# A cross-attention kernel: queries projected once and scattered by small transfers, keys sent by thirds

## The chip, the cores and the metric

One core of one Trainium2 chip runs the whole program. The metric is the device time of one execution in microseconds (us), median of several. The engines are TensorE (PE), VectorE (DVE), ScalarE (ACT), GpSimd (POOL) and SyncE (SP), which here only issues transfers.

## The reference, cut to what matters

```python
def _L0_xattn_ref(Q, K, V, mask, W_q, W_k, W_v, W_o):     # 32 batches, 100 queries, 1444 keys, width 128, 16 heads of 8
    q = (Q @ W_q.T).reshape(B, -1, 16, 8).transpose(0, 2, 1, 3)
    k = (K @ W_k.T).reshape(B, -1, 16, 8).transpose(0, 2, 1, 3)
    v = (V @ W_v.T).reshape(B, -1, 16, 8).transpose(0, 2, 1, 3)
    scores = jnp.einsum('bhqd,bhkd->bhqk', q, k) / np.sqrt(8)
    attn = masked_softmax(scores, m)                      # clip to +-50, exp, mask, divide by the sum
    out = jnp.einsum('bhqk,bhkd->bhqd', attn, v)
    ...
x = x + _L0_xattn_ref(_layernorm(x), ctx_1024, ctx_1024, mask, W_q, W_k, W_v, W_o)
x = x + _L0_ffn_ref(_layernorm(x), gate_w, w1, w2)        # 8 experts of width 512, the best two of each token
```

## The kernel before

**Batches and chunks.** The attention runs over 32 batches. The keys of a batch lie in 12 tiles of 128, the heads in 4 groups of 4; a group of one tile gives scores of 128 keys x 400 (4 heads x 100 queries). Three such blocks make a chunk, so a batch has 16 chunks, numbered c = 0 to 15. For each chunk PE makes the scores into one of two PSUM halves (line 689), ACT takes the exponential (line 899), and DVE clips it (`clip`, line 1047). On every even chunk PE also runs 24 matmuls that weigh the values with the clipped exponentials of earlier chunks (`weigh_values`, line 701); odd chunks have none.

**The steps between.** After the scores of each chunk PE does one step of `STEPS`, which all go through one PSUM bank, `scratch`. A step may start only when ACT or DVE has emptied the bank of the step before (`scratch_emptied`). During batch b the steps prepare batch b+1 (`PREPARE`: query, turn and key for each third of the keys, value for each third) and finish batch b-1 (`FINISH`: heads, queries, project, tokens, gate, rank). The order before is turn, key, turn, key, turn, key, heads, queries, project, query, value, tokens, gate, value, value, rank, in chunks 0 to 15. So turn steps stand in even chunks, followed by the 24 matmuls, and key steps in odd ones. PE runs in order: a step that waits holds up the scores behind it.

**Scores from split operands.** The score matmuls read the type fp32r. Each operand is split by DVE into a rounded part and a rest (`split_keys`, `split_queries`), and the four products of the parts are summed by stacking them along the 128 rows of the contraction: 4 terms x 4 heads x 8. The keys get there by transfer: `stack_keys` issues 16 transfers of 192 KB per batch on SP's queue (line 405), one for each term and group, once all three thirds are split. The queries are projected four times over, from a weight in which each group's columns are repeated for the four terms (`wq_rep`, `project_q`, line 624: four matmuls, which the profile shows as eight instructions). POOL then multiplies them with `head_mask`, which leaves each row only its own head's columns, and writes `q_stack`, 128 x 1600 (`stack_queries`, line 505).

**Who waits for the stacks.** The scores of chunk 0 of the next batch are made in chunk 15 of this one. Ahead of them PE waits for `q_stacked` and for all 16 transfers of `k_stacked`. SP's order in a batch is: wait for all scores of the batch before, load the context for two batches on, fill rows of the expert buffer (line 397), wait for the three key splits, send the 16 transfers. Ahead of batch 0 the same is done alone (`ALONE`, `first_keys`), and `xT` is built from normalised tokens.

POOL's other work in a batch is small: line 560 and 562 (the deviation of the second norm), which DVE waits for two chunks after project, and the sending of routed rows by indirect transfers (line 570), which follows rank. DVE takes the gate's logits at line 1100.

After the attention come the experts, 57 tiles of 128 rows, and the final sums; the diff leaves them alone.

## Time and profile before

| | |
|---|---|
| median of 3 runs | 1222.54 us (1222.02 to 1223.01) |
| profiled execution, its own time | 1220.12 us |
| its span | 1218.4 us |
| PE / DVE / ACT / POOL busy | 1074.9 / 860.4 / 753.7 / 366.9 us |
| transfers on SP's queue | 84084 packets, 152.55 MB |
| POOL's stack of the queries (L505) | 32 times, 107.4 us busy |

The span runs from the first to the last instruction of the profiled execution; its own time holds 1.7 us more. Busy times of different engines overlap, so they don't add up to the span. In a timeline "x8" merges eight instructions in a row, "[1.37 <-X]" is the idle time of that engine just before, and what ended it. The busy time of a matmul includes its way through the array, so that neighbours overlap by some 0.15 us; the distance between two starts is what an instruction group takes on PE.

### The profile page before, as it was taken

What the parts mean: (1) busy time and instruction counts of PE and PEld (TensorE: products, weight loads), DVE (VectorE), ACT (ScalarE), POOL (GpSimd) and SP (SyncE); (2) the same over time, 40 slices, a digit from 0 to 9 for tenths busy, and PEclk for the clock granted to TensorE, in tenths of its full rate; (3) what the DMA queues carried; (4) which work ended last, traced back from release to release, by engine and by line L of the source; (5) the groups of instructions that cost most, each with busy time, mean ns of one, the idle gap of its engine ahead of it and who ended that gap; (6) DMA issues with size and microseconds to landing.
All of it is one profiled execution on the core that took longest, in us unless ns stands there. A gap on an engine that the chain in (4) does not pass through costs nothing.

```text
span 1218.4 us, 30948 instructions
## 1 busy us (share of the span) xinstructions
PE 1074.9 (88%) x10734; PEld 778.3 (64%) x10735; DVE 860.4 (71%) x1955; ACT 753.7 (62%) x959; POOL 366.9 (30%) x357
## 2 busy tenths in 40 slices
PE   5699999999999999999999999999999999869990
PEld 3466666666666666666666666666666666569990
DVE  4567777777777777777777777777777777644443
ACT  2576666666666676766666766666666666634440
POOL 3712222222222222222222222222222222235554
PEclk8799999999999999999999999999999999979995
DMA  6655666666555665555555556666666666312225
GB/s 157 144 125 137 143 146 145 145 144 139 133 131 135 145 145 135 134 134 134 134 134 134 132 133 138 145 145 145 145 145 137 134 135 141 113 48 66 68 57 162
DMA packets 89010, 159.58 MB, mean 131 GB/s; under 512 B 13792, under 2 KB 66020, under 8 KB 88980
## 3 DMA queue, kind: packets, MB, share of 16 engines
q1 hardware_dynamic: 84084, 152.55, 54.3%
q0 software_dynamic: 4896, 6.63, 2.0%
q8 instruction: 18, 0.29, 0.1%
q14 instruction: 12, 0.10, 0.0%
HBM read 36.83 MB, written 22.08 MB: 48 GB/s over the span
## 4 chain that ended last, share of the span: by engine, by line
PE 64%; DVE 17%; ACT 5%; issue 5%; SPq 4%; DMA 4%; ACTq 0%; DVEq 0%; POOL 0%; POOLq 0%
PE o_sum L701 17%; PE scores L689 15%; DVE probs L1047 12%; PE scratch L618 6%; PE scratch L632 6%; PE scratch L613 5%; ACT k_full L866 4%; PE scores L805 4%; PE scores L816 4%; SPq L405 3%; PE scratch L624 2%; DVE v_both L983 2%; PE scratch L662 2%; DMA k_stack<-k_lo 2%; DMA x_all<-in_x_dram 1%
## 5 line engine op out<-in xcount | busy, mean ns | idle before, releaser
L899 ACT ACTIVATE probs<-scores 128x1200 f32<-128x1200 f32 x512 | 589.5, 1179 | 114.9 <-PE scores L689 114.9
L1047 DVE TENSOR_SCALAR probs<-probs 128x1200 f32<-128x1200 f32 x512 | 471.2, 947 | 52.9 <-ACT probs L899 50.4
L689 PE MATMUL scores<-q_stack,k_stack 128*128 128x400 f32 x1536 | 431.3, 395 | 13.4 <-DMA k_stack<-k_lo 11.3
L689 PEld LDWEIGHTS scores<-q_stack,k_stack 128*128 128x128 f32 x1536 | 255.8, 190 | 141.6 <-issue 98.3
L701 PE MATMUL o_sum<-probs,v_both 128*17 128x200 f32 x6144 | 309.8, 334 | 0.1
L701 PEld LDWEIGHTS o_sum<-probs,v_both 128*17 128x17 f32 x6144 | 154.8, 97 | 84.1 <-issue 16.5
L632 PE MATMUL scratch<-w_turned,ctxT 128*128 128x128 f32 x768 | 112.0, 289 | 56.0 <-DVE logits L1100 41.3
L570 POOL DMA_INDIRECT expert_rows<-rows,row_atu x64 | 79.0, 1235 | 264.0 <-DVE row_atu L1140 238.2
L632 PEld LDWEIGHTS scratch<-w_turned,ctxT 128*128 128x128 f32 x768 | 93.8, 192 | 87.3 <-DVE logits L1100 51.3
L505 POOL TENSOR_TENSOR q_stack<-q_parts,head_mask 128x1600 fp32r<-128x1600 f32 x32 | 107.4, 3357 | 96.9 <-DVE q_parts L970 96.9
L560 POOL TENSOR_SCALAR rstd<-moments 100x1 f32<-100x1 f32 x32 | 39.0, 1220 | 279.5 <-DVE moments L1085 279.5
L866 ACT COPY k_full<-scratch 128x512 f32<-128x512 f32 (+1 forms) x93 | 52.1, 560 | 92.0 <-PE scratch L618 92.0
L618 PE MATMUL scratch<-ctxT,w_turned 128*128 128x512 f32 x186 | 91.1, 571 | 0.0
L957 DVE CAST k_hi<-k_full 128x512 fp32r<-128x512 f32 (+1 forms) x93 | 38.9, 419 | 58.1 <-ACT k_full L866 58.1
L983 DVE COPY v_both<-scratch 128x512 f32<-128x512 f32 x93 | 64.1, 689 | 17.0 <-PE scratch L632 14.8
L596 POOL DMA_INDIRECT expert_outputs<-ctx_nat,tile_home x57 | 56.8, 997 | 61.7 <-DVE ctx_nat L1249 60.1
L959 DVE TENSOR_TENSOR k_lo<-k_full,k_hi 128x512 fp32r<-128x512 f32 (+1 forms) x93 | 61.4, 660 | 3.2
L805 PE MATMUL scores<-ctxT 128*128 128x128 f32 x456 | 61.7, 279 | 0.0
L816 PE MATMUL scores<-w_sb,k_full 128*128 x456 | 60.9, 276 | 0.1
L930 ACT ACTIVATE k_full<-scores 128x512 f32<-128x512 f32 x57 | 34.0, 597 | 38.0 <-PE scores L805 37.4
L805 PEld LDWEIGHTS scores<-ctxT 128*128 128x128 f32 x456 | 56.6, 195 | 0.3
L816 PEld LDWEIGHTS scores<-w_sb,k_full 128*128 128x128 f32 x456 | 55.5, 192 | 0.5 <-issue 0.5
(145 smaller groups left out, 869.8 us busy)
## 6 DMA issues: line engine op xcount, KB each, us to landing
k_stack<-k_hi SPq DMA_DIRECT2D x256, 192.0 KB, 4.6
k_stack<-k_lo SPq DMA_DIRECT2D x256, 192.0 KB, 5.4
expert_rows<-fill SPq DMA_DIRECT2D x32, 406.2 KB
xT_and_ctx<-in_ctx_dram SPq DMA_DIRECT2D x16, 704.0 KB
ctx_nat<-in_ctx_dram SPq DMA_DIRECT2D x16, 704.0 KB
v_both<-expert_rows SPq DMA_DIRECT2D x57, 65.0 KB, 1.8
xT_and_ctx<-in_L_ffn_w_dram SPq DMA_DIRECT2D x1, 2048.0 KB, 11.7
w_sb<-in_L_ffn_w_dram SPq DMA_DIRECT2D x8, 256.0 KB, 7.1
```

Source lines behind the costliest of these rows:

```text
L505: nc.gpsimd.tensor_tensor(q_stack[p][:], q_parts[:].bitcast(F32).unsqueeze(2).broadcast_to([P, GROUPS, HG, SQ]), head_mask[:].unsqueeze(1) ...
L570: nc.gpsimd.indirect_dma_start(out=expert_rows[0:E * CAP, :], out_offset=bass.IndirectOffsetOnAxis(ap=row_atu[:, k:k + 1], axis=0), in_=ro ...
L618: return nc.tensor.matmul(into[:, 0:KEYS[k]], w_turned[:, WK, :], ctxT[:, KEY_COLS[k]], start=True, stop=True)
L632: last = nc.tensor.matmul(scratch[:, j * P:(j + 1) * P], ctxT[:, t * P:(t + 1) * P], w_turned[:, WV, :], start=True, stop=True)
L689: last = nc.tensor.matmul(scores[:, c % 2, m, 0:GQ], k_stack[p][:, g, t * P:(t + 1) * P], q_stack[p][:, g, :, :].rearrange("p h q -> p (h ...
L701: last = nc.tensor.matmul(o_sum[32 * g:32 * g + VW, s * PQ:(s + 1) * PQ], v_ones[p][:, t, 2 * g + s, :], probs[:, c % RING, m, s * PQ:(s + ...
L805: last = nc.tensor.matmul(scores[:, n % 2, 0, c * P:(c + 1) * P], w1_tile[:, n % 2, c * P:(c + 1) * P], tileT[:, n % 2, :], start=True, st ...
L816: last = nc.tensor.matmul(scores[:, n % 2, 1, 0:D], hiddenT[:, n % 2, c, :], w2_sb[:, bass.ds(expert, 1), c, :].rearrange("f o d -> f (o d)"),
L866: nc.scalar.copy(k_full[:, k, 0:KEYS[k]], scratch[:, 0:KEYS[k]]).then_inc(scratch_emptied, 1)
L899: nc.scalar.activation(probs[:, c % RING, :, :], scores[:, c % 2, :, 0:GQ], ACT.Exp, scale=SCALE).then_inc(exp_ready, 1)
L983: nc.vector.tensor_copy(v_ones[p][:, k * KC:(k + 1) * KC, :, 0:2 * DH], scratch[:].rearrange("p (t n d) -> p t n d", t=KC, n=PAIRS)).then_ ...
L1047: nc.vector.tensor_scalar(chunk, chunk, LOW, HIGH, ALU.max, ALU.min).then_inc(probs_ready, 1)
```

## The change

The queries are projected once, 128 x 100, and split in two parts (`q_parts`, 128 x 2 x 100). `q_stack` is zeroed once by POOL, and 16 transfers of 12.5 KB (8 rows of 4 x 100 numbers, in pieces of 400 bytes) write the blocks that aren't zero. POOL's product, `head_mask` and `wq_rep` go. With it goes an order of columns in which one transfer takes a term for all groups: the columns of `W_q` and `W_k` are put in the order head, place in the head, group when ACT copies the turned weights. The keys are sent a third at a time, 4 transfers of 256 KB in pieces of 2 KB, each third as soon as it is split and with a semaphore of its own; PE waits for the second and third in the chunks that first need them. The query step moves from chunk 9 to chunk 0. The order is then query, turn, key, turn, key, turn, key, heads, queries, project, value, value, tokens, gate, value, rank.

```diff
@@ constants
-    KD = 16 * 4 * GROUPS
+    KD = 16 * 4
+    QD = 16 * 4 * HG
...
-    STEPS = (PREPARE[1:7] + FINISH[:3] + PREPARE[:1] + PREPARE[7:8] + FINISH[3:5] + PREPARE[8:] + FINISH[5:])
+    STEPS = PREPARE[:7] + FINISH[:3] + PREPARE[7:9] + FINISH[3:5] + PREPARE[9:] + FINISH[5:]
@@ SP
-            def stack_keys(p):
+            def stack_keys(p, b):
                 R = HG * DH
-                for t, part in enumerate((k_hi, k_lo, k_hi, k_lo)):
-                    for g in range(GROUPS):
-                        sp.dma_start(k_stack[p][t * R:(t + 1) * R, g, :].bitcast(F32),
-                                     part[g * R:(g + 1) * R, :].bitcast(F32)).then_inc(k_stacked, 16)
+                for k in range(KSTEPS):
+                    sp.wait_ge(k_split, KSTEPS * b + k + 1)
+                    cols = slice(k * KC * P, (k + 1) * KC * P)
+                    for t, part in enumerate((k_hi, k_lo, k_hi, k_lo)):
+                        sp.dma_start(k_stack[p][t * R:(t + 1) * R, :, cols].bitcast(F32),
+                                     part[:, cols].bitcast(F32)).then_inc(k_stacked[k], 16)
+            def stack_queries(p):
+                R = GROUPS * DH
+                for t in range(4):
+                    for h in range(HG):
+                        first = t * HG * DH + h * DH
+                        sp.dma_start(q_stack[p][first:first + DH, :, h, :].bitcast(F32),
+                                     q_parts[h * R:(h + 1) * R, t // 2, :].bitcast(F32)).then_inc(q_stacked, 16)
             sp.wait_ge(cleared, 3)
-            sp.wait_ge(k_split, KSTEPS)
-            stack_keys(0)
+            stack_keys(0, 0)
+            sp.wait_ge(q_stack_cleared, 2)
+            sp.wait_ge(q_split, 1)
+            stack_queries(0)
...
                 fill_rows(b + 1)
-                sp.wait_ge(k_split, KSTEPS * (b + 2))
-                stack_keys(1 - p)
+                sp.wait_ge(q_split, b + 2)
+                stack_queries(1 - p)
+                stack_keys(1 - p, b + 1)
@@ POOL
-            nc.gpsimd.memset(own_head[:], 1.0).then_inc(own_head_step, 1)
...
+            for p in range(2):
+                nc.gpsimd.memset(q_stack[p][:].bitcast(F32), 0.0).then_inc(q_stack_cleared, 1)
...
-            def stack_queries(p, b):
...
-                nc.gpsimd.tensor_tensor(
-                    q_stack[p][:], q_parts[:].bitcast(F32).unsqueeze(2).broadcast_to([P, GROUPS, HG, SQ]),
-                    head_mask[:].unsqueeze(1).unsqueeze(3).broadcast_to([P, GROUPS, HG, SQ]), ALU.mult
-                ).then_inc(q_stacked, 1)
@@ PE
-                for g in range(GROUPS):
-                    last = nc.tensor.matmul(scratch[:, g * SQ:(g + 1) * SQ],
-                                            wq_rep[:, g, :, :].rearrange("p t r -> p (t r)"),
-                                            xT[:, cols], start=True, stop=True)
+                last = nc.tensor.matmul(scratch[:, 0:SQ], w_turned[:, WQ, :], xT[:, cols], start=True, stop=True)
...
+                        for k in range(1, KSTEPS):
+                            if c + 1 == k * KC * GROUPS // CB:
+                                pe.wait_ge(k_stacked[k], KD * (b + 1))
                         score_chunk(p, c + 1)
                     elif not last_one:
-                        pe.wait_ge(q_stacked, b + 2)
-                        pe.wait_ge(k_stacked, KD * (b + 2))
+                        pe.wait_ge(q_stacked, QD * (b + 2))
+                        pe.wait_ge(k_stacked[0], KD * (b + 2))
@@ ACT
-            nc.scalar.copy(w_turned[:].rearrange("p n d -> p (n d)"), scores[:, 1, 2, :]
+            nc.scalar.copy(w_turned[:, 0:2, :].rearrange("p n (h d g) -> p n h d g", h=HG, d=DH),
+                           scores[:, 1, 2, 0:2 * P].rearrange("p (n g h d) -> p n h d g", n=2, g=GROUPS, h=HG))
+            nc.scalar.copy(w_turned[:, 2:4, :].rearrange("p n d -> p (n d)"), scores[:, 1, 2, 2 * P:4 * P]
...
-            nc.scalar.copy(wq_rep[:], w_turned[:, WQ, :].rearrange("p (g r) -> p g r", g=GROUPS)
...
-                    nc.scalar.copy(q_full[:], scratch[:, 0:GROUPS * SQ]).then_inc(scratch_emptied, 1)
+                    nc.scalar.copy(q_full[:], scratch[:, 0:SQ]).then_inc(scratch_emptied, 1)
@@ DVE
-                    dve.wait_ge(k_stacked, KD * b)
+                    dve.wait_ge(k_stacked[k], KD * b)
...
-                    dve.wait_ge(q_stacked, b)
-                flat = q_parts[:].rearrange("p g q -> p (g q)")
-                nc.vector.tensor_copy(flat, q_full[:]).then_inc(q_hi_ready, 1)
+                    dve.wait_ge(q_stacked, QD * b)
+                nc.vector.tensor_copy(q_parts[:, 0, :], q_full[:]).then_inc(q_hi_ready, 1)
                 dve.wait_ge(q_hi_ready, b + 1)
-                nc.vector.tensor_tensor(flat[P // 2:P, :], q_full[P // 2:P, :],
-                                        flat[P // 2:P, :].bitcast(F32), ALU.subtract
+                nc.vector.tensor_tensor(q_parts[:, 1, :], q_full[:], q_parts[:, 0, :].bitcast(F32), ALU.subtract
                                         ).then_inc(q_split, 1)
```

## Rows read from the trace of the kernel before

**Rows 1.** The page: busy time of each engine over the whole span.

```profile
PE 1074.9 (88%) x10734; PEld 778.3 (64%) x10735; DVE 860.4 (71%) x1955; ACT 753.7 (62%) x959; POOL 366.9 (30%) x357
```

**Rows 2.** Busy time by stretch: PE, PEld, DVE, ACT, POOL, then PE clock, DMA share, GB/s.

```profile
23.00:40.80 17.80, 5.63 (x24) 4.79 (x25) 12.91 (x72) 2.06 (x4) 13.54 (x17) 0.50 0.95 206
587.00:619.00 32.00, 29.65 (x307) 20.59 (x306) 24.62 (x52) 21.78 (x26) 8.42 (x7) 1.00 0.60 138
```

**Rows 3.** Timeline of PE over one batch: start us, us, engine, line, operation.

```profile
577.71 0.25 PE L671 MATMUL scratch<-ident,rows 100*128 100x100 f32 x1
...
581.88 1.16 PE L632 MATMUL scratch<-w_turned,ctxT 128*128 128x128 f32 x8 [1.37 <-DVE logits L1100]
...
583.95 1.16 PE L632 MATMUL scratch<-w_turned,ctxT 128*128 128x128 f32 x8 [0.36 <-DVE v_both L983]
585.04 1.21 PE L701 MATMUL o_sum<-probs,v_both 128*17 128x200 f32 x24
...
586.83 0.26 PE L682 MATMUL scratch<-chosen,before 100*100 100x8 f32 x2
...
587.75 0.60 PE L613 MATMUL scratch<-ident,xT_and_ctx 128*128 128x128 f32 x4
...
590.07 1.02 PE L618 MATMUL scratch<-ctxT,w_turned 128*128 128x512 f32 x2
...
591.84 0.66 PE L613 MATMUL scratch<-ident,xT_and_ctx 128*128 128x128 f32 x4 [0.20 <-ACT k_full L866]
...
599.98 0.65 PE L662 MATMUL scratch<-ident,o_raw 128*100 128x128 f32 x4
...
603.01 0.38 PE L667 MATMUL scratch<-w_turned,attnT 128*100 128x128 f32 x2
...
605.12 1.03 PE L624 MATMUL scratch<-xT_and_ctx,wq_rep 128*128 x8
...
606.80 1.16 PE L632 MATMUL scratch<-w_turned,ctxT 128*128 128x128 f32 x8
...
609.68 0.25 PE L671 MATMUL scratch<-ident,rows 100*128 100x100 f32 x1
```

**Rows 4.** The waits: us in total, times, longest.

```profile
PE scratch L632 <- DVE logits L1100: 41.3, 30, 1.4
```

**Rows 5.** Timeline of DVE, then of POOL, in the same batch.

```profile
577.62 4.14 DVE L1047 TENSOR_SCALAR probs<-probs 128x1200 f32<-128x1200 f32 x2
...
601.17 0.36 DVE L1064 TENSOR_TENSOR attn<-scratch,rden 100x64 f32<-100x64 f32 x2
...
577.75 3.37 POOL L505 TENSOR_TENSOR q_stack<-q_parts,head_mask 128x1600 fp32r<-128x1600 f32 x1 [2.93 <-DVE q_parts L970]
```

**Rows 6.** Line 1047 alone: duration in ns, min/median/max.

```profile
L1047 DVE TENSOR_SCALAR probs<-probs x512: 752/779/3439, 43.5 to 1057.2; 128x1200 f32<-128x1200 f32 x171
```

**Rows 7.** Timeline of ACT in the same batch.

```profile
588.39 0.58 ACT L862 COPY ctxT<-scratch 128x512 f32<-128x512 f32 x1
```

**Rows 8.** Timeline of the lead-in, all engines.

```profile
9.82 0.23 POOL L515 TENSOR_SCALAR rstd<-moments 100x4 f32<-100x4 f32 x1 [6.72 <-DVE moments L1005]
...
19.85 0.69 DVE L993 TENSOR_TENSOR k_lo<-scores,k_hi 128x512 fp32r<-128x512 f32 x1
...
23.08 2.53 SPq L405 DMA_DIRECT2D k_stack<-k_hi  x4
...
28.70 0.57 DVE L970 TENSOR_TENSOR q_parts<-q_full,q_parts 64x400 fp32r<-64x400 f32 x1
...
32.35 2.92 SPq L405 DMA_DIRECT2D k_stack<-k_lo  x4
...
40.83 1.67 PE L689 MATMUL scores<-q_stack,k_stack 128*128 128x400 f32 x4 [10.44 <-DMA k_stack<-k_lo]
```

**Rows 9.** Lines 397 and 384 on SP's queue: one issue in ns; issue to landing.

```profile
L397 SPq DMA_DIRECT2D expert_rows<-fill x32: 315/324/1120, 36.0 to 999.5; - x32
...
DMA to landing us min/median/max: 1.8/2.0/2.1
```

More of the change, by code:

```diff
@@ L163, in xattn_moe @@
         w_turned = sb("w_turned", [P, 4, P])
-        wq_rep = sb("wq_rep", [P, GROUPS, 4, HG * DH])
-        q_parts = sb("q_parts", [P, GROUPS, SQ], F32R)
-        own_head = sb("own_head", [P, 4, HG])
-        head_mask = sb("head_mask", [P, HG])
+        q_parts = sb("q_parts", [P, 2, SQ], F32R)
         q_stack = [sb(f"q_stack{p}", [P, GROUPS, HG, SQ], F32R) for p in range(2)]
@@ L176, in xattn_moe @@
         k_full = sb("k_full", [P, KSTEPS, KC * P])
-        q_full = sb("q_full", [P, GROUPS * SQ])
+        q_full = sb("q_full", [P, SQ])
         k_hi = sb("k_hi", [P, TILES * P], F32R)
@@ L282, in xattn_moe @@
         xT_ready = sem("xT_ready")
-        wq_rep_ready = sem("wq_rep_ready")
-        own_head_step = sem("own_head_step")
-        head_mask_ready = sem("head_mask_ready")
+        q_stack_cleared = sem("q_stack_cleared")
         q_hi_ready = sem("q_hi_ready")
@@ L293, in xattn_moe @@
         q_split = sem("q_split")
-        k_stacked = sem("k_stacked")
+        k_stacked = [sem(f"k_stacked{k}") for k in range(KSTEPS)]
         scores_ready = sem("scores_ready")
@@ L489, in _ @@
                                     base=0, pattern=[[-1, P]], channel_multiplier=1).then_inc(ident_ready, 1)
-            nc.gpsimd.memset(own_head[:], 1.0).then_inc(own_head_step, 1)
-            pool.wait_ge(own_head_step, 1)
-            nc.gpsimd.affine_select(out=own_head[:], in_=own_head[:], compare_op=ALU.is_ge, fill=0.0, base=0,
-                                    pattern=[[-HG * DH, 4], [-DH, HG]], channel_multiplier=1
-                                    ).then_inc(own_head_step, 1)
-            pool.wait_ge(own_head_step, 2)
-            nc.gpsimd.affine_select(out=own_head[:], in_=own_head[:], compare_op=ALU.is_ge, fill=0.0, base=DH - 1,
-                                    pattern=[[HG * DH, 4], [DH, HG]], channel_multiplier=-1
-                                    ).then_inc(own_head_step, 1)
-            def stack_queries(p, b):
-                pool.wait_ge(q_split, b + 1)
-                if later(b, 2):
-                    pool.wait_ge(scores_ready, CHUNKS * (b - 1))
-                nc.gpsimd.tensor_tensor(
-                    q_stack[p][:], q_parts[:].bitcast(F32).unsqueeze(2).broadcast_to([P, GROUPS, HG, SQ]),
-                    head_mask[:].unsqueeze(1).unsqueeze(3).broadcast_to([P, GROUPS, HG, SQ]), ALU.mult
-                ).then_inc(q_stacked, 1)
+            for p in range(2):
+                nc.gpsimd.memset(q_stack[p][:].bitcast(F32), 0.0).then_inc(q_stack_cleared, 1)
             pool.wait_ge(half_ready, 1)
@@ L537, in _ @@
                 invert_deviations(r)
-            pool.wait_ge(head_mask_ready, 1)
-            stack_queries(0, 0)
             for r in range(DVE_NORMS, QSTEPS):
@@ L576, in during @@
                     invert_deviation(b - 1)
-                if not (isinstance(b, int) and b == B - 1):
-                    stack_queries(1 - p, b + 1)
                 if later(b):
@@ L730, in _ @@
                     pe.wait_ge(xT_ready, 1)
-                    pe.wait_ge(wq_rep_ready, 1)
                 into_scratch(name, k, 0, 0, None, step)
@@ L735, in _ @@
             pe.wait_ge(mask_ready, 1)
-            pe.wait_ge(q_stacked, 1)
-            pe.wait_ge(k_stacked, KD)
+            pe.wait_ge(q_stacked, QD)
+            pe.wait_ge(k_stacked[0], KD)
             score_chunk(0, 0)
@@ L847, in _ @@
                 nc.scalar.copy(ctxT[:, KEY_COLS[k]], scores[:, 0, k, 0:KEYS[k]]).then_inc(ctxT_ready, 1)
-            act.wait_ge(w_turned_ready, 1)
-            nc.scalar.copy(wq_rep[:], w_turned[:, WQ, :].rearrange("p (g r) -> p g r", g=GROUPS)
-                           .unsqueeze(2).broadcast_to([P, GROUPS, 4, HG * DH])).then_inc(wq_rep_ready, 1)
             def take(name, k, b, f, step):
@@ L1017, in _ @@
             nc.vector.tensor_copy(mask_rows[:], mask_u8[:]).then_inc(mask_cast, 1)
-            dve.wait_ge(own_head_step, 3)
-            nc.vector.tensor_reduce(head_mask[:], own_head[:].rearrange("p t h -> p h t"), AX.X, ALU.add
-                                    ).then_inc(head_mask_ready, 1)
             moments_of(0)
```

## The prediction

> **What bounds the kernel now.** I read the page first. PE is busy for 88% of the span, the next engine for 71% [rows 1], so the question is what PE does in the rest. The windows come second: a steady stretch of 32 us holds 29.65 us of PE at a granted clock of 1.00, that is at the 2.4 GHz level, and the transfer engines are busy for 0.60 of it [rows 2]. So PE bounds the attention, but 2.35 us of each stretch are stalls. Third comes PE's timeline, where the reader should look at distances between starts. The batch repeats from 577.71 to 609.68, so a period is 31.97 us [rows 3]. The largest stall is 1.37 us ahead of a value step, because the gate's logits hadn't been taken from `scratch`; the waits have it 30 times, 41.3 us in all [rows 3, 4].
>
> Why is DVE late with the logits? Its two clips at 577.62 take 4.14 us together. POOL's product for the query stack runs from 577.75 to 581.12, inside them [rows 5]. The middle clip takes 779 ns and the longest 3439 ns [rows 6]: two undisturbed ones would be 1.56 us, so 2.6 us are lost while POOL works, and the first DVE work behind them is the logits. The stall on PE is DVE's loss less the slack that the 24 matmuls of the even chunk give.
>
> **Part 1: POOL's product goes.** The clips fall back to 0.78 us each, and the logits are taken about 2.6 us sooner. That is more than the stall, so all of it goes: 1.37 us in the idle column, or 1.52 by distances. I find the latter so: tokens to value was 581.88 - 577.71 = 4.17 us, and the work in it is one even gap and one odd gap. What an even chunk adds after its step is the 24 matmuls and the next scores: 586.83 - 585.04 = 1.79 us. The 24 matmuls alone are 1.14 (1.21 less their overlap), so the scores are 0.65. With 0.21 for the small tokens and gate matmuls the work is 1.79 + 0.65 + 0.21 = 2.65, and the stall 1.52 [rows 3].
>
> **Part 2: one projection in place of four.** Query to value is 606.80 - 605.12 = 1.68 us: 0.65 scores, some 0.81 of query matmuls, the rest a stall for ACT's copy [rows 3]. A quarter of the matmuls is 0.20 us (0.26 if a quarter of the busy 1.03 counts). ACT's copy and DVE's split shrink too, but lie beside PE's work.
>
> **Part 3: the order of the steps.** Moving query to chunk 0 shifts turn, key, heads, queries and project by one chunk, so each changes between even (covered by the 24 matmuls) and odd (covered by scores alone). I go round the new batch and compare gap by gap [rows 3, 7].
> - Turn to heads, before: 599.98 - 587.75 = 12.23 us. Now turn is odd. Its matmuls take 0.60, ACT's copy starts 0.11 later and takes 0.58 [rows 7], and 0.05 later PE may go on: 1.33 against 0.53 + 0.65 = 1.18 of work, a stall of 0.15. Key is even, and its copy is covered: the stall of 0.20 ahead of each turn goes. A pair is 1.33 + 0.9 (key) + 1.79 = 4.02, twice, and 3.81 for the shorter third: 11.85.
> - Heads to project, before 603.01 - 599.98 = 3.03. Heads is now odd, and DVE's reciprocal and two products of the heads (0.65 us in a row up to 601.53 [rows 5]) with 0.2 of hand-over are longer than the 0.65 of scores. I take a stall of 0.28: 0.57 + 0.65 + 0.28 + 0.02 + 1.79 = 3.31.
> - Project to value, before 606.80 - 603.01 = 3.79 with query in it. Now project is odd: 0.31 + 0.65 + 0.14 of stall = 1.10. Query in chunk 0 is 0.20 + 1.79 = 1.99. Together 3.09.
> - The first value step to the next step is 609.68 - 606.80 = 2.88, as before.
> - From there to the last value step, before 6.24 (4.17 + 583.95 - 581.88 = 2.07 for an odd value step with its stall). Now the odd value step comes first, 2.07, then tokens and gate without the stall, 2.65: 4.72.
> - The last value step to rank 2.88 and rank to the next batch 0.92, both as before.
>
> Before: 12.23 + 3.03 + 3.79 + 2.88 + 6.24 + 2.88 + 0.92 = 31.97, the period. After: 11.85 + 3.31 + 3.09 + 2.88 + 4.72 + 2.88 + 0.92 = 29.65 us. The difference is 2.32 us per batch, made of about 1.5 for POOL, 0.6 for the projection and 0.2 from the rest.
>
> One dependence gets shorter: rank needs `chosen`, which DVE now makes one chunk before it. Behind the last value step DVE copies values (0.7), picks (0.6), and PE has 1.79 until rank: just enough. The share of the gate is now taken by ACT in chunk 15, behind an exponential that by then is done. If it were late, DVE would hold rank, and PE the query step of the next batch.
>
> **Part 4: the transfers.** The 16 query transfers are new on SP's queue. An issue costs 0.32 us when nothing holds it [rows 9], and 2.92 / 4 = 0.73 us among key transfers [rows 8]: 5 to 12 us per batch. The 12 key transfers carry the same 3 MB at 9 to 11 us. With the context and the rows (1 us) SP has 15 to 24 us of issues in 29.65. The queries go first, in chunk 1, the last keys after chunk 7, near 15 us: sent by 19, landed by 26 even with 7 us of landing. Chunk 0 of the next batch needs only the first third, and the last third isn't wanted before chunk 10. So I cost them at nothing. What hides them is PE's batch itself; if the queue ran full, the excess over 29.65 us would be paid. DVE's waits for `q_stacked` and `k_stacked[k]` before it overwrites the parts concern transfers one batch old.
>
> The pieces of a query transfer are 400 bytes, and no SBUF-to-SBUF transfer of such pieces is in the trace; the expert buffer's rows of 520 bytes go in pieces as small and are issued at 0.32 us [rows 9]. I take them as cheap and keep the other end as a rival. The Trainium skill, DMA: Bandwidth & Descriptors, section Bandwidth, says that transfers under 64 KB are descriptor-dominated and gives each a fixed cost of about 2 us. If these costs added up, 16 of them would be 32 us per batch, as an estimate from that page, longer than a batch; the trace speaks against adding them up, for the four weight loads of 64 KB, issued in a row, each landed within 2.1 us of its issue [rows 9].
>
> **Part 5: the lead-in.** PE stands 10.44 us before its first scores, at a clock of 0.50 (the 1.2 GHz level) and with the transfer engines 0.95 busy at 206 GB/s [rows 2, 8]. The keys are sent from 23.08; by thirds they can start at 19.85 + 0.69 = 20.54, so the last key transfer is issued near 32.9 instead of 35.3. Behind it SP issues 16 query transfers (their split is ready by 29.3), 5.1 us at best and 11.7 at worst, and they land 2 us later: first scores at 40 to 46.6 us instead of 40.83 [rows 8, 9]. The keys at least thin out by then; I take 41.5, a loss of 0.7. The two clearings of `q_stack` cost at most a product of the same size each, 6.7 us together, and lie in POOL's idle 6.72 us ahead of 9.82 [rows 5, 8]; cover gone, they would delay that line by a few us once.
>
> **The sum.** The POOL stall is there in 30 batches [rows 4], so I take 30 x 2.32 = 69.6 us. Batch 0 gives about 1 (the projection and half a stall), the last batch prepares nothing. 69.6 + 1 - 0.7 = 70 us. The profiled execution's own time of 1220.1 becomes 1150, and the median of the runs, 1222.5, which is 2.4 above it, becomes 1152.5. I round down to 1152.
>
> **The rivals.**
> - Odd steps drain slower than I reckon. The one odd step with a measured drain by DVE, the value step, stalls PE for about 0.5 us. If turn (three times), heads and project each stalled so, instead of 0.15, 0.15, 0.09, 0.28 and 0.14, that is 1.7 us more per batch, 51 in all: 1203. With half of it 1177. For it: DVE and ACT are both busy for two thirds. Against: DVE loses 2.6 us of waiting. Chance 0.12 for a gain between 20 and 50 us.
> - POOL's product isn't the cause of the slow clips, and something else, such as the key transfers that run at the same time, is. Then only the projection and the order count, 0.8 us per batch: 1222.5 - 25 = 1197. Against: the clip ends with POOL's product and not with the transfers. Chance 0.03.
> - PE loses nearly all stalls: 29.65 less 1.2 is 28.4 us, another 36 us: 1116. Chance 0.06 for anything below 1135.
> - It ends slower: small transfers occupy the queue one after the other. A 64 KB transfer lands 1.8 to 2.1 us after its issue [rows 9]; if each of the 16 held the queue for 1.8 us, they would take 29 us, with 9 for keys and 3 for the context and rows 41 us per batch: 9 us more than before, 31 batches, 1500. It decides from 1.2 us each: 16 x 1.2 + 12 = 31 us. Chance 0.04.
> - No change within 0.2% (2.4 us, about what this measurement can tell): gain and new stalls cancel, 2.3 us of new stalls per batch. Chance 0.02.
>
> **How the numbers follow.** The forecast as described, 1135 to 1172, has 0.73. Leaving out 2 in 10 of all cases, I take 1134 to 1176, which takes in the lead-in's bounds (-1 to +6), the query matmuls' (0.06 x 31 = 2 us), and a third of the first rival. Faster 0.94, same 0.02, slower 0.04.
>
> **What the profile after would show.** Line 1047's longest instruction near 1 us instead of 3.4. No wait of PE for the logits of 41 us. The query step as two instructions right behind rank. A period of 29 to 30.3 us between two value steps. Stalls of 0.1 to 0.3 us ahead of the key steps for ACT's copy, where they stood ahead of turn. No wait of PE on `k_stack` or `q_stack` outside the lead-in. The first scores at 40 to 47 us. I would be wrong if the key step waited for a copy that stands behind an exponential, if rank came late because `chosen` is made one chunk before it, or if SP were still issuing query transfers when the keys are split.

## The result, and the profile after

The changed kernel takes 1331.46 us (median of 4 runs, 1328.71 to 1335.89) where the kernel before takes 1222.28 beside it: a ratio of 1.0899 (95% interval 1.0883 to 1.0915), slower by 9%. The forecast was 1152, in a range of 1134 to 1176. The profiled execution has a span of 1326.7 us at a mean granted clock of 0.917 (1 is the 2.4 GHz level); before they were 1218.4 and 0.972.

A period (the distance between the first and the last of the 14 context loads of one buffer, divided by the 26 batches between them) was (939.2 - 106.6) / 26 = 32.02 us and is (1035.1 - 114.0) / 26 = 35.43. So 30 batches lost 102 us, and the first scores, at 51.54 us instead of 40.83, another 10.7: together 113, where the runs lost 109 (1331.46 - 1222.28).

The page of the changed kernel: busy time of each engine; then its chain that ended last, by engine and by line; then its key transfers (how many, KB each, median us from issue to landing).

```profile
PE 1117.3 (84%) x10542; PEld 792.0 (60%) x10543; DVE 754.8 (57%) x1954; ACT 755.6 (57%) x959; POOL 255.5 (19%) x324
...
SPq 49%; DMA 23%; PE 17%; issue 5%; DVE 5%; ACT 0%; POOL 0%; DVEq 0%; POOLq 0%; ACTq 0%
...
k_stack<-k_hi SPq DMA_DIRECT2D x192, 256.0 KB, 11.6
k_stack<-k_lo SPq DMA_DIRECT2D x192, 256.0 KB, 13.1
```

Against [rows 1] DVE lost 106 us of work and POOL 111, as the change intends. But the chain now runs through SP's queue (`SPq`, the issuing of transfers) and the transfers themselves for 72% of the span, and through PE for 17%, where it was 64% before. PE's busy time even rose by 42 us with fewer matmuls. The waits of PE (us in total, times, longest) say what it waits for:

```profile
PE scores L675 <- DMA k_stack<-k_lo: 96.9, 30, 5.1
PE scores L675 <- DMA q_stack<-q_parts: 22.6, 1, 22.6
```

The wait for the logits of [rows 4] is gone; 96.9 us for the first third of the next batch's keys stand in its place. SP's timeline over one batch and the start of the next shows why they are late (L412 issues queries, L403 keys, L373 the context):

```profile
577.46 20.90 SPq L412 DMA_DIRECT2D q_stack<-q_parts  x16
598.49 0.59 SPq L403 DMA_DIRECT2D k_stack<-k_hi  x1
...
605.72 0.63 SPq L403 DMA_DIRECT2D k_stack<-k_lo  x1
611.30 0.37 SPq L373 DMA_DIRECT2D xT_and_ctx<-in_ctx_dram  x1
...
614.37 18.82 SPq L412 DMA_DIRECT2D q_stack<-q_parts  x16
633.32 0.59 SPq L403 DMA_DIRECT2D k_stack<-k_hi  x1
```

The 16 query issues occupy SP for 18.8 to 20.9 us, and the keys go only then: in the second batch shown DVE had split the first third by 621.85 and the last by 628.20, and SP sent them from 633.32 on. The chain resolves these 16 issues one by one:

```profile
577.46 10.14 SPq L412
587.65 0.71 SPq L412
...
600.42 8.74 DMA k_stack<-k_lo
609.21 1.37 PE scores L675 x3
614.37 2.50 SPq L412
616.91 6.28 SPq L412
623.24 0.67 SPq L412
```

One issue is held for 10.14 us (two, for 2.50 and 6.28, in the next batch); the others follow each other at a distance of 0.71. And the fourth key transfer, the last of the first third, takes 8.74 us to land. Windows of the changed kernel (busy time of PE, PEld, DVE, ACT and POOL, then PE clock, DMA share, GB/s; the share is the mean busy share of the 16 transfer engines and can read a little over 1):

```profile
606.00:611.00 5.00, 1.79 (x8) 1.74 (x8) 0.00 (x0) 0.30 (x1) 0.00 (x0) 0.81 1.08 125
611.00:614.40 3.40, 3.40 (x30) 2.26 (x29) 2.84 (x12) 2.20 (x3) 1.17 (x2) 0.50 1.10 123
618.00:624.00 6.00, 5.87 (x64) 3.42 (x64) 4.41 (x8) 4.98 (x7) 0.00 (x0) 1.00 1.12 127
624.00:630.00 6.00, 5.81 (x54) 3.69 (x56) 3.89 (x9) 4.73 (x8) 0.51 (x2) 1.00 0.84 222
```

Two things are to be seen. The transfer engines are fully busy and move 123 to 127 GB/s, where the lead-in before had 206 at a share of 0.95 [rows 2]. The 3 MB of a batch's keys take 25 us at that rate, by estimate; sent from 598.49 they are through near 623.5. The held query issue goes on at 623.24, and the last window has 222 GB/s: the keys are gone by then. And after PE's stall of 4.05 us the clock falls to the 1.2 GHz level (0.50), where the steady stretch before has 1.00. This is where PE's extra busy time comes from: the same 10542 matmuls are busy for 1060.4 us in experiment 1, which has no such stalls.

So keys and queries follow each other: some 25 us of key traffic until the queries are let in (598.49 to 623.24), then 10.1 us of query issues (623.24 to 633.32) until the keys are let in. From one batch's first key issue to the next these are 34.83 us, in the batch after it 35.37 (633.32 to 668.69), against a measured mean period of 35.43.

### The profile page after: what moved, and what is told of

Read it like the earlier page. It is cut to its first block, busy times and chain, and to the rows that moved or that the text cites. A ratio compares the mean times of both kernels' runs of the same rounds, so it can differ in the third digit from the quotient of the medians.

```text
span 1326.7 us, 31018 instructions
## 1 busy us (share of the span) xinstructions
PE 1117.3 (84%) x10542; PEld 792.0 (60%) x10543; DVE 754.8 (57%) x1954; ACT 755.6 (57%) x959; POOL 255.5 (19%) x324
## 4 chain that ended last, share of the span: by engine, by line
SPq 49%; DMA 23%; PE 17%; issue 5%; DVE 5%; ACT 0%; POOL 0%; DVEq 0%; POOLq 0%; ACTq 0%
SPq L412 43%; DMA k_stack<-k_lo 20%; SPq L403 5%; PE scores L675 4%; PE scores L793 4%; PE scores L804 4%; PE o_sum L687 1%; DVE probs L1028 1%; DMA x_all<-in_x_dram 1%; SPq L474 1%; DMA q_stack<-q_parts 1%; PE scratch L669 1%; DVE q_parts L955 1%; DVE q_parts L953 1%; PE scores L783 0%
## 5 line engine op out<-in xcount | busy, mean ns | idle before, releaser
L675 PE MATMUL scores<-q_stack,k_stack 128*128 128x400 f32 x1536 | 436.1, 396 | 120.9 <-DMA k_stack<-k_lo 96.9
L1028 DVE TENSOR_SCALAR probs<-probs 128x1200 f32<-128x1200 f32 x512 | 388.9, 781 | 82.5 <-ACT probs L885 81.8
L675 PEld LDWEIGHTS scores<-q_stack,k_stack 128*128 128x128 f32 x1536 | 265.7, 202 | 216.9 <-DMA k_stack<-k_lo 107.3
L687 PE MATMUL o_sum<-probs,v_both 128*17 128x200 f32 x6144 | 334.0, 353 | 0.5 <-issue 0.4
L687 PEld LDWEIGHTS o_sum<-probs,v_both 128*17 128x17 f32 x6144 | 161.1, 101 | 149.9 <-issue 84.2
L618 PE MATMUL scratch<-w_turned,ctxT 128*128 128x128 f32 x768 | 105.7, 281 | 1.9 <-ACT v_both L874 0.7
L848 ACT COPY ctxT<-scratch 128x512 f32<-128x512 f32 (+1 forms) x93 | 52.2, 561 | 95.1 <-PE scratch L602 95.1
L607 PE MATMUL scratch<-ctxT,w_turned 128*128 128x512 f32 x186 | 99.7, 618 | 7.4
L1033 DVE COPY o_raw<-o_sum 128x400 f32<-128x400 f32 x32 | 18.4, 575 | 120.0 <-PE o_sum L687 120.0
L545 POOL COPY rows<-home 100x2 f32<-100x2 f32 x32 | 10.3, 320 | 345.7 <-DMA expert_rows<-rows,row_atu 322.6
L551 POOL TENSOR_SCALAR rstd<-moments 100x1 f32<-100x1 f32 x32 | 19.2, 599 | 191.6 <-DVE moments L1066 191.6
## 6 DMA issues: line engine op xcount, KB each, us to landing
q_stack<-q_parts SPq DMA_DIRECT2D x512, 12.5 KB
```

The source lines that it names most:

```text
L607: return nc.tensor.matmul(into[:, 0:KEYS[k]], w_turned[:, WK, :], ctxT[:, KEY_COLS[k]], start=True, stop=True)
L618: last = nc.tensor.matmul(scratch[:, j * P:(j + 1) * P], ctxT[:, t * P:(t + 1) * P], w_turned[:, WV, :], start=True, stop=True)
L675: last = nc.tensor.matmul(scores[:, c % 2, m, 0:GQ], k_stack[p][:, g, t * P:(t + 1) * P], q_stack[p][:, g, :, :].rearrange("p h q -> p (h ...
L687: last = nc.tensor.matmul(o_sum[32 * g:32 * g + VW, s * PQ:(s + 1) * PQ], v_ones[p][:, t, 2 * g + s, :], probs[:, c % RING, m, s * PQ:(s + ...
L1028: nc.vector.tensor_scalar(chunk, chunk, LOW, HIGH, ALU.max, ALU.min).then_inc(probs_ready, 1)
```

## The experiments

Ratios are against the kernel before, run beside it on the same chip, with 95% intervals; the chips differ between experiments, so compare ratios and not times. "Period" is as above. Line numbers shift a little between kernels. A "wait for `k_stack`" is a wait of PE before its scores until keys have landed.

**1. The changed kernel without its query transfers in the loop.** Both stacks are filled once, with the queries of batch 0, so later batches use wrong queries; all else is as in the changed kernel.

```
+            stack_queries(1)
...
-                sp.wait_ge(q_split, b + 2)
-                stack_queries(1 - p)
```

> The changed kernel without the 16 query transfers of each batch (both query stacks are filled once, from batch 0's queries, so all later scores use the wrong queries; everything else runs). In the changed kernel SP spends 18.8 to 20.9 us of each batch on these issues and sends the keys only behind them. Theory A (the query transfers hold the queue and push the keys behind the start of the next batch): PE's waits on k_stack outside the lead-in go from 97 us to under 5, the period falls from 36 us to 29.5 to 30.5, the run to 1150 to 1175 us. Theory B (the keys in pieces of 2 KB are slow by themselves, 24 us of transfers per batch, and fill the batch whatever the queries do): the waits on k_stack stay above 40 us and the run above 1250.

Measured: 1185.88 us, 0.9666 (0.9646 to 0.9685), period 30.23, no wait of PE for `k_stack`, although keys still take a median of 9.8 us from issue to landing (12.3 in the changed kernel). Without the query issues the slow keys harm nobody. The period is the one that theory A gave; the time is 11 us above its range. Some 4 us of that are the lead-in: 32 query transfers are issued there instead of 16, and the first scores come at 55.62 us instead of 51.54. This also isolates the forecast of PE's work: 30.23 against 29.65.

**2. Keys by thirds on the kernel before.** 12 transfers, each from 128 partitions into 32, as in the changed kernel; queries and order as before.

```
+                for k in range(KSTEPS):
+                    sp.wait_ge(k_split, KSTEPS * b + k + 1)
...
+                        sp.dma_start(k_stack[p][t * R:(t + 1) * R, :, cols].bitcast(F32),
+                                     part[:, cols].bitcast(F32)).then_inc(k_stacked[k], 16)
```

> The kernel before with one part of the change alone: the keys by thirds, 12 transfers of 256 KB in pieces of 2 KB (and the columns of W_k in the order they need). POOL's product, four projections and the old order stay. Theory B: the key transfers run at about 125 GB/s here too, where 16 transfers in pieces of 6 KB run at 215, so transfers are busy for over 0.8 of a batch; PE doesn't notice, because the first third goes 8 us earlier: 1190 to 1225 us. Theory A's stronger form (the slow rate is caused by the small query transfers beside them): the rate stays above 190 GB/s, the transfer share at 0.6, 1190 to 1222 us. The rate tells them apart, not the time.

Measured: 1219.03, 0.9928 (0.9911 to 0.9946), period 32.13. The same window columns, for this kernel:

```profile
630.00:640.00 10.00, 9.92 (x120) 7.41 (x114) 7.69 (x16) 7.10 (x10) 3.45 (x3) 1.00 1.08 136
```

136 GB/s with engines at 1.08 and no query transfer anywhere: the rate belongs to the form of the key transfers. So it isn't the small query transfers beside them. The period didn't gain; the first scores came 3 us earlier (37.80).

**3. Keys in 4 whole transfers.** On the changed kernel: the same 128 partitions into 32, but pieces of 6 KB, sent after the third split.

```
+                sp.wait_ge(k_split, KSTEPS * (b + 1))
...
+                    sp.dma_start(k_stack[p][t * R:(t + 1) * R, :, :].bitcast(F32),
+                                 part[:, :].bitcast(F32)).then_inc(k_stacked, 16)
```

> The changed kernel with each term's keys in one transfer of 768 KB in pieces of 6 KB, sent once all three thirds are split (4 transfers; rows still come from all 128 partitions). If the length of the pieces sets the rate: 215 GB/s, 15 us for 3 MB, the query issues aren't held (16 x 0.71 = 11.4 us); the keys are split about 16 us after chunk 15's scores and land 16 us later, so the period is 32 to 34 us and the run 1220 to 1270. If what slows them is that the rows of one transfer come from 128 partitions: 125 GB/s as in the changed kernel, 24 us from the split to the landing, a period near 41 us and 1400 to 1500.

Measured: 1731.77, 1.4111 (1.4086 to 1.4136), period 47.81, beyond what either theory allowed (the mean granted clock is 0.821). A window:

```profile
655.00:662.00 7.00, 4.97 (x65) 3.59 (x65) 4.49 (x14) 3.65 (x5) 0.00 (x0) 1.00 1.05 115
```

Three times longer pieces don't help, nor do three times larger transfers: 115 GB/s. PE waits 439.4 us for the keys, 28 times.

**4. Keys in 16 whole transfers.** As 3, with the transfers of the kernel before, each from 32 partitions into 32.

```
+                    for g in range(GROUPS):
+                        sp.dma_start(k_stack[p][t * R:(t + 1) * R, g, :].bitcast(F32),
+                                     part[g * R:(g + 1) * R, :].bitcast(F32)).then_inc(k_stacked, 16)
```

> The changed kernel with the keys sent as before: 16 transfers of 192 KB in pieces of 6 KB, each from 32 partitions to 32, once all thirds are split. Both readings of the slow rate expect 215 GB/s here. Theory B in full (only the slow keys hurt, the query transfers are free): 1190 to 1215. Theory A and B together (query issues of 11.4 us ahead of the keys, and the keys land 32 to 33 us after chunk 15's scores): 1225 to 1270.

Measured: 1341.43, 1.0924 (1.0904 to 1.0944), period 35.35. A window, then SP's timeline:

```profile
640.00:646.00 6.00, 5.76 (x70) 4.25 (x70) 4.37 (x9) 3.02 (x5) 1.58 (x2) 1.00 1.03 209
```
```profile
622.07 11.88 SPq L411 DMA_DIRECT2D q_stack<-q_parts  x16
634.65 2.57 SPq L402 DMA_DIRECT2D k_stack<-k_hi  x4
...
643.06 3.08 SPq L402 DMA_DIRECT2D k_stack<-k_lo  x4
```

The rate is back (209 GB/s), and the query issues are no longer held: 11.88 us for 16. The time isn't, and lies above both expectations, for another reason: the third split ends at 634.63, the keys are issued at once, until 646.14, and the next scores start 5.8 us later, at 651.98. The cure of the rate was joined to a wait for all thirds, so this run shows the rate and the hold, and not the price.

**5. The new order alone**, on the kernel before.

```
-    STEPS = (PREPARE[1:7] + FINISH[:3] + PREPARE[:1] + PREPARE[7:8] + FINISH[3:5] + PREPARE[8:] + FINISH[5:])
+    STEPS = PREPARE[:7] + FINISH[:3] + PREPARE[7:9] + FINISH[3:5] + PREPARE[9:] + FINISH[5:]
```

> The kernel before with the new order of the steps alone (query in chunk 0). The fourth run's reading is that with the keys sent whole, a chain binds: scores of chunk 0, third split, 16 transfers one behind the other, next scores. Before it took 14.8 + 16.3 = 31.1 us, just under PE's 31.97. The new order puts the third split one chunk later, by 2 us: 33 to 34 us per batch and 1255 to 1290 us, with PE waiting for k_stack or q_stack's semaphores in each batch. Rival (the order costs nothing, as the prediction had it, and the query transfers were what made the fourth run slow): 1205 to 1225.

Measured: 1295.69, 1.061 (1.0589 to 1.0631), period 34.10. Its timelines of DVE, PE and POOL:

```profile
615.95 3.69 DVE L1047 TENSOR_SCALAR probs<-probs 128x1200 f32<-128x1200 f32 x1
...
620.81 0.43 PE L671 MATMUL scratch<-ident,rows 100*128 100x100 f32 x1 [2.33 <-DVE v_both L983]
...
616.16 2.84 POOL L505 TENSOR_TENSOR q_stack<-q_parts,head_mask 128x1600 fp32r<-128x1600 f32 x1
```

The expectation was wrong in its cause, and low in its range: PE waits for `k_stack` only 4 times in the loop, 4.7 us in all. POOL's product stands in POOL's program behind `rstd`, which needs the project step. So it doesn't run right behind the query step in chunk 0, but behind project; it slows a clip ahead of a value copy now, and PE waits 2.33 us for that copy at tokens (69.9 us in 30 times). The clock falls to 0.56 behind it, where 24 matmuls take 2.20 us instead of 1.21. In the kernel before, the order isn't neutral, but what made it dear is POOL's product, which the change removes: with the product on DVE and the keys by thirds the new order costs 0.17 us per batch (experiment 10).

**6. The product on DVE**, on the kernel before, as four instructions of 128x400 each.

```
+                for h in range(HG):
+                    ins = nc.vector.tensor_scalar(q_stack[p][:, :, h, :], q_parts[:].bitcast(F32),
+                                                  head_mask[:, h:h + 1], None, ALU.mult)
```

> The kernel before with the product of the query stack made by DVE, in four instructions of 128 x 400, one for each head of a group, in place of POOL's one. If POOL's product is what stretches the two clips (prediction, part 1): no clip over 1.5 us, PE's wait for the logits goes from 41 us to under 5, and the period falls until the key chain of 31.1 us binds: 1190 to 1207. If something else stretches the clips: they stay at 3.4 us and the run at 1222 or above, since DVE has 1.5 us more work.

Measured: 1220.93, 0.9994 (0.9978 to 1.001), period 32.02: no change. Its line of the clips (duration in ns, min/median/max), then PE's longest wait:

```profile
L1040 DVE TENSOR_SCALAR probs<-probs x512: 751/778/1035, 44.3 to 1058.0; 128x1200 f32<-128x1200 f32 x171
```
```profile
PE scores L674 <- DMA k_stack<-k_lo: 39.1, 29, 10.5
```

The cause of the slow clips is shown: nothing but POOL's product was moved, and the longest clip falls from 3439 ns [rows 6] to 1035. The wait for the logits goes too. But the time stays, above the 1190 to 1207 expected. All keys are still sent after the third split (in one batch from 603.68 until 614.87, and the scores that need them start at 620.70), and PE now waits for them where it had waited for the logits: 10.5 us in the lead-in and 28.6 in 28 batches. A second chain lay directly under the first.

**7. Experiment 6 with keys by thirds** in 12 transfers, as in 2.

> The sixth run's kernel, and the keys by thirds in 12 transfers of 256 KB from 128 partitions. Both bounds are taken away: the lock and the key chain. Period 30.2 to 30.8, transfers busy over 0.9 of it at 125 GB/s in the key stretches: 1165 to 1190 us. If the transfers then bind (24 us of keys, 5 us of context and rows, and they rarely start at once), PE waits for k_stack and it stays at 1195 or above.

Measured: 1181.47, 0.9669 (0.9652 to 0.9687), period 30.80, no wait for `k_stack`. Both are as expected. Thirds and the product's removal are each worth nearly nothing (0.7%, and 0.1% within the noise) and together 3.3%.

**8. Experiment 6 with keys by thirds in 48 transfers** of 64 KB, 32 partitions into 32, pieces of 2 KB as in the changed kernel.

```
+                        for g in range(GROUPS):
+                            sp.dma_start(k_stack[p][t * R:(t + 1) * R, g, cols].bitcast(F32),
+                                         part[g * R:(g + 1) * R, cols].bitcast(F32)).then_inc(k_stacked[k], 16)
```

> As the seventh, but each third in 16 transfers of 64 KB, each from 32 partitions to 32, in pieces of 2 KB; 48 per batch. If it is the spread of a transfer's rows over 128 partitions that halves the rate: above 185 GB/s in the key stretches, transfer share about 0.65, no wait for k_stack, 1165 to 1190 us. If it is the length of the pieces: 125 GB/s again. If the issues of 48 transfers on SP's queue cost 0.6 us each (29 us), SP binds: 1200 or more.

Measured: 1306.4, 1.0685 (1.0666 to 1.0705), period 34.59. A window, and the key issues (ns, min/median/max):

```profile
625.00:630.00 5.00, 4.37 (x47) 3.18 (x46) 4.60 (x16) 4.07 (x5) 0.00 (x0) 1.00 0.42 105
```
```profile
L408 SPq DMA_DIRECT2D k_stack<-k_hi x768: 507/591/2306, 22.3 to 1128.1; - x192
```

105 GB/s with engines at 0.42 is 250 GB/s while they are busy: pieces of 2 KB are not slow, the spread over partitions is. SP, at 0.62 us for each of 48 issues, is the bound now, the third of the outcomes expected: DVE waits 130.0 us, in 32 times, for the key transfers before it may overwrite `k_hi`, and PE waits for DVE. The Trainium skill, DMA: Bandwidth & Descriptors, section Why small descriptors are slow (HBM only), says that transfers between SBUF places don't suffer from small pieces; by that rule, this trace agrees, for pieces of 2 KB.

**9. The changed kernel with its query transfers issued by POOL's own queue**, in loop and lead-in.

```
-                        sp.dma_start(q_stack[p][first:first + DH, :, h, :].bitcast(F32),
+                        nc.gpsimd.dma_start(q_stack[p][first:first + DH, :, h, :].bitcast(F32),
```

> The changed kernel with its 16 query transfers issued by POOL on its own queue instead of SP's; nothing else changes. SP then sends each third of the keys when it is split. If it was their place on SP's queue that cost the time (0.67 us of SP each, and the first one held up by the key transfers before it): no wait for k_stack outside the lead-in, period 30 to 31 us as without the queries (1185.9), run 1170 to 1205. If the transfer engines, busy for 0.9 of a batch with the slow form of the keys, are what the query transfers overload: waits for k_stack or q_stack stay and the run is 1230 or more.

Measured: 1195.17, 0.9747 (0.9726 to 0.9767), period 30.85, no wait for `k_stack`. POOL's timeline:

```profile
611.00 9.94 POOL L496 DMA_DIRECT2D q_stack<-q_parts  x16
```

The same bytes in the same pieces cost 0.62 us per batch against no query transfers at all (30.85 against 30.23) when they don't stand between the keys on one queue, and 5.2 when they do. PE waits for `q_stack` in four batches of the loop, 9.6 us in all.

**10. Experiment 7 with the new order.**

> The seventh run's kernel (product by DVE, keys by thirds in 12 transfers) in the new order of the steps. The order cost 74 us in the fifth run. If that was only the key chain, which the thirds take away, it costs nothing here, and by the prediction's gaps it gives 0.2 us per batch: 1168 to 1185 against 1181.5. If odd steps drain slower than reckoned (the prediction's first rival): 1190 to 1230.

Measured: 1189.45, 0.9705 (0.9676 to 0.9733), period 30.97 against 30.80. The time falls between the two expectations. The intervals of this ratio and of experiment 7's overlap; the gain of 0.2 us per batch that the prediction gave the order isn't there.

**11. Experiment 7 with keys in 24 transfers** of 128 KB, each from 64 partitions into 32.

```
+                        for g in range(0, GROUPS, 2):
+                            sp.dma_start(k_stack[p][t * R:(t + 1) * R, g:g + 2, cols].bitcast(F32),
+                                         part[g * R:(g + 2) * R, cols].bitcast(F32)).then_inc(k_stacked[k], 16)
```

> The seventh run's kernel with two transfers of 128 KB per term and third, each from 64 partitions to 32 (24 per batch, about 15 us of issues). The rate was 215 to 250 GB/s from 32 partitions and 125 from 128. If it falls with the number of source partitions per target partition: 150 to 190 GB/s when the engines are full, transfer share 0.6 to 0.8. The time is PE's either way: 1175 to 1190.

Measured: 1184.13, 0.9655 (0.9634 to 0.9676), period 30.82, with this rate:

```profile
612.00:616.00 4.00, 3.92 (x43) 3.04 (x38) 2.74 (x7) 2.76 (x4) 1.83 (x2) 1.00 1.10 173
```

173 GB/s lies between the 115 to 136 of 128 partitions and the 209 of 32. The size of a transfer doesn't explain this: 128 KB went at 173 here, 192 KB at 209 (experiment 4) and 256 KB at 136 (experiment 2). Where keys don't bind, it is worth nothing.

**12. The changed kernel with keys in 24 transfers**, as in 11; the query transfers stay on SP ahead of the keys.

> The changed kernel with the keys in two transfers of 128 KB per term and third, each from 64 partitions to 32 (24 per batch), which ran at 170 GB/s instead of 125; the 16 query transfers stay on SP's queue, ahead of the keys. If the loss needs both parts, the query issues and the backlog of slow key transfers that holds the first of them for 10 us, then the queries take 12 us here and not 19 to 21, SP has 12 + 15 + 1 us of issues, just under a batch, and the period is 30 to 31.5 us: 1195 to 1235. If the query transfers ahead of the keys suffice by themselves: PE waits for k_stack by 2 us or more in each batch and the run is 1270 or above.

Measured: 1182.5, 0.967 (0.9654 to 0.9686), period 30.48. SP's timeline, and PE's wait:

```profile
606.42 11.93 SPq L413 DMA_DIRECT2D q_stack<-q_parts  x16
618.49 1.22 SPq L404 DMA_DIRECT2D k_stack<-k_hi  x2
...
632.61 1.25 SPq L404 DMA_DIRECT2D k_stack<-k_lo  x2
634.33 0.36 SPq L373 DMA_DIRECT2D ctx_nat<-in_ctx_dram  x1
```
```profile
PE scores L676 <- DMA k_stack<-k_lo: 12.1, 21, 0.7
```

The form of the key transfers alone turns +9% into -3.3%, a version that beats both kernels, and 12 us better than the lower end of what was expected. The bytes of the keys and the length of their pieces are those of the changed kernel, only the rate isn't, and the queries are hardly held any more (11.93 us, 13.04 in the next batch; the longest single issue is 2.51 us instead of 10.58). But SP issues for 11.9 + 15.4 + 1 of every 30.5 us, and PE still waits 0.6 us in 21 batches: this version has little room left on its queue.

**13. Experiment 12 with the lead-in's 16 query transfers issued by ACT.**

```
+                    nc.scalar.dma_start(q_stack[0][first:first + DH, :, h, :].bitcast(F32),
+                                        q_parts[h * R:(h + 1) * R, t // 2, :].bitcast(F32)).then_inc(q_stacked, 16)
```

> The twelfth run's kernel with the 16 query transfers of the lead-in alone issued by ACT, which has nothing to do there; in the loop they stay on SP. If the late start is their place behind the keys on SP's queue: first scores at 41 to 44 us instead of 50.4, and the run at 1172 to 1177 against 1182.5. If SP's 29.5 us of issues per batch bind as much as PE, SP is relieved by 12 us as well, so this doesn't eat the gain. If the engines themselves are the limit in the lead-in (keys of 3 MB ahead of everything): first scores after 48 us and 1179 or more.

Measured: 1185.33, 0.9672 (0.9655 to 0.9689), period 30.65, so nothing gained, as the last of the three expectations had it. The first scores come at 48.39 instead of 50.42: ACT takes 12.32 us for the 16 issues, and they land 6.3 us later. The lead-in's lateness is only in small part their place behind the keys on SP's queue. What the rest is, the engines full of keys or the transfers themselves, stays open; a context load of 704 KB is also issued sooner here, at 38.46 instead of 49.81, and competes with the queries.

## Why the prediction was wrong

**Part 4 failed, the transfers costed at nothing.** Two sentences of it carry the error. "The 12 key transfers carry the same 3 MB at 9 to 11 us": the bytes are the same, but each transfer now gathers from 128 partitions into 32, and they go at 125 GB/s, 25 us (experiments 2 and 3; not the pieces' length, experiments 3 and 8; with 32 partitions 209, with 64 it is 173). What I took for the transfer, 9 to 11 us, was the time of the issues. And the query issues, costed at 0.32 to 0.73 us each, "5 to 12 us per batch": unheld, 16 take 11.5 to 11.9 us, the upper bound; but they are issued while the last batch's keys are still in flight and are held for 8 to 10 us first. (The prediction's estimate of 32 us from fixed costs that add up isn't borne out. The figure of about 2 us stands in the Trainium skill, DMA: Bandwidth & Descriptors, in the section Anatomy of one DMA — SWDGE (gpsimd) path, for transfers that GpSimd issues, and not in the section Bandwidth.) Each error alone would have been hidden: slow keys without query issues give 30.23 (experiment 1), query issues with faster keys 30.48 (experiment 12), both on separate queues 30.85 (experiment 9). Together they form a ring of 34.8 to 35.4 us: late keys hold the next queries, and these the next keys. The prediction named the form of it, "if SP were still issuing query transfers when the keys are split", and "if the queue ran full, the excess over 29.65 us would be paid". The excess is 35.43 - 29.65 = 5.78 us per batch, 173 us in 30, and with the lead-in's 10 that makes 183, where 179 lie between forecast and result. Of the 5.78 the ring is 5.2 (35.43 against 30.23 in experiment 1), and 0.58 is PE's own work (Part 3).

**The fourth rival was the right one, at the wrong size.** It said that the small transfers occupy the queue one after the other, "decides from 1.2 us each". Held and unheld together an issue cost 18.8 / 16 = 1.18 to 20.9 / 16 = 1.31 us. It wasn't 1.8, so the time was 1331 and not 1500; and the 1.2 isn't a cost of the small transfer but 0.71 of its own and the rest from the keys ahead of it. With the keys at 9 us the rival priced the wrong half.

**Part 1 was right.** The longest clip and the missing wait for the logits are as foretold. Line 1028, duration in ns:

```profile
L1028 DVE TENSOR_SCALAR probs<-probs x512: 751/778/1045, 54.2 to 1163.5; 128x1200 f32<-128x1200 f32 x171
```

Experiment 6 shows POOL's product as the cause, and rules the second rival out. The Trainium skill, SBUF — State Buffer, section Who interferes with whom, tells of a port that VectorE and GpSimd share under a lock; by that rule, the clips here agree: 3439 ns beside a product of 3.37 us [rows 5, 6], 1035 without it. What Part 1 left out is the chain underneath: alone, its 1.5 us are worth nothing, since the keys sent as a whole then bind at 32.02 (experiment 6).

**Part 2** was right that the query step is two instructions. From its start to that of the 24 matmuls it takes 0.38 us in experiment 1 (601.37 to 601.75) where I took 0.20, so of the 0.6 us it gave about 0.4. No run isolates it.

**Part 3** was reasoned on gaps that nothing else moves. In experiment 1, which has PE's work of the changed kernel undisturbed, one batch measured 12.80 us from turn to heads (forecast 11.85), 3.37 to project (3.31), 0.96 to value (1.10), 2.17 for query to turn (1.99), and each other gap within 0.25 of its forecast, 30.51 in all against 29.65. The term that is off is turn to heads, by 0.95. The first key step stands like this in PE's timeline of that kernel:

```profile
605.41 1.12 PE L606 MATMUL scratch<-ctxT,w_turned 128*128 128x512 f32 x2 [0.72 <-ACT ctxT L847]
```

PE stood 0.72 us instead of the 0.15 that I took, for the copy `ctxT` that ACT makes. The two turns behind it drained as forecast, so the turns together cost 0.4 us more. The other 0.5 is the key steps, each 0.15 to 0.21 longer from its start to that of the 24 matmuls than the 0.9 (0.69 for the shorter third) of the sum; their matmuls of 128x512 are busy for a mean of 643 to 644 ns in the new order (experiments 1 and 10) and 592 to 599 in the old (the kernel before and experiment 6). Why is open. That is the first rival (odd steps drain slower) in small and only in part, 0.6 us per batch by the period, 17 us in all. Experiment 10 agrees: the order gives nothing. That `chosen` comes one chunk before rank cost nothing, as I had it.

**Part 5**: the first scores came at 51.54 us; I took 41.5 out of 40 to 46.6. The issues came as reckoned (keys from 20.70, queries until 40.60); the landing was wrong, 11 us instead of 2. "The keys at least thin out by then" was said of keys at the old rate; at the new one 25 us of them start at 20.70, and the window behind the last query issue is still full of them:

```profile
40.60:46.00 5.40, 0.00 (x0) 0.00 (x0) 0.00 (x0) 0.00 (x0) 5.21 (x8) 0.50 1.08 127
46.00:51.50 5.50, 0.00 (x0) 0.00 (x0) 0.00 (x0) 0.00 (x0) 1.96 (x5) 0.50 0.99 177
```

That this is the whole reason is argued, not shown (experiment 13).

## What to carry to other kernels

Price a transfer between SBUF places twice, by its issue and by its partitions: the same bytes in fewer transfers that gather from more partitions ran at about half the rate here, and the time from issue to landing must be measured for the new form. Add up, for one period and one queue, the issues and the backlog that an issue meets, and ask what stands behind them. A removed stall pays only down to the next chain; here the two edits that were worth nothing alone (experiments 2 and 6) were worth 3.3% together.

## What the runs showed of the hardware

- The more partitions a transfer gathered into 32, the slower it went, with the engines fully busy (share 1.03 to 1.10): 32 gave 209 GB/s, 64 gave 173, 128 gave 115 to 136. Neither the length of the pieces (2 or 6 KB) nor the size of a transfer (128 to 768 KB) orders these rates. Why is not shown.
- An issue of a transfer between SBUF places took SP some 0.6 to 0.7 us (medians 0.59 for 64 KB, 0.67 for 12.5 KB; 0.60 for one of 256 KB); loads of the context and fills took 0.32 to 0.38. A query transfer's issue took a median of 0.55 from POOL's queue and 0.68 from ACT's.
- An issue was held while the queue's transfers were backed up: for 10.14 us in the batch shown, for 10.58 at most. Behind the lead-in's 12 key transfers alone the queries weren't held (16 in 11.89 us, though the engines were full); in the loop a context load and a fill lay ahead of them too. How much has to lie ahead isn't shown.
- Behind a stall of PE of 4.05 us the granted clock was 0.50 for 3.4 us, and by 618 it was back at 1.00. Behind one of 2.33 us it was 0.56 (experiment 5); behind one of 1.89 us, in the next batch of the changed kernel, it stayed at 1.00.
